# Two samples of a stream through one expert layer at a time, and an order of layers across the samples

## What is computed

```python
x = x + L0_attn(ln(x))   # layer 0: state space scan, 16 heads   (SSM below)
x = x + L0_ffn(ln(x))    # layer 1: feed-forward, token shift     (FFN)
x = x + L1_attn(ln(x))   # layer 2: mamba block, 16 states        (MAM)
x = x + L1_ffn(ln(x))    # layer 3: 8 experts, top 2, gelu        (MOE1)
x = x + L2_attn(ln(x))   # layer 4: linear attention              (ATT)
x = x + L2_ffn(ln(x))    # layer 5: ternary feed-forward          (TER)
x = x + L3_attn(ln(x))   # layer 6: selective scan                (SCAN)
x = x + L3_ffn(ln(x))    # layer 7: 8 experts, top 2, gated silu  (MOE3)
```

## Time and profile before

| | us |
|---|---|
| median of 3 runs | 1499.15 |
| lowest, highest | 1498.88, 1500.82 |
| profiled execution, its own time | 1508.51 |
| profiled execution, span from first to last instruction | 1506.4 |
| PE busy, DVE busy, ACT busy, POOL busy in the span | 1151.1, 920.1, 662.9, 280.6 |

### The profile page before, as it was taken

How to read it: one execution, slowest core, us unless ns; L and a number is a source line. 1 busy time by engine, 2 the same in 40 slices (tenths; PEclk the granted TensorE clock), 3 DMA queues, 4 the chain that set the end, 5 groups by cost and what they waited for, 6 DMA issues and landing times.

```text
span 1506.4 us, 16451 instructions
## 1 busy us (share of the span) xinstructions
PE 1151.1 (76%) x5428; PEld 761.0 (51%) x5428; DVE 920.1 (61%) x2079; ACT 662.9 (44%) x1289; POOL 280.6 (19%) x261
## 2 busy tenths in 40 slices
PE   0988656667869989976897767755867999978774
PEld 0534522233757446666775423433635745547674
DVE  4575679998627384234484778987786355334432
ACT  1532267524634343452452476436943434443321
POOL 1200112425140201203202211213242020020222
PEclk9998767877989998989999868986988999988987
DMA  8000000003564000536540000003513600033763
GB/s 330 0 1 0 1 0 0 0 1 103 188 200 125 20 1 4 172 101 212 172 166 28 7 0 0 0 1 104 172 43 104 200 15 1 0 131 121 271 205 131
DMA packets 57641, 125.50 MB, mean 83 GB/s; under 512 B 5320, under 2 KB 38224, under 8 KB 57168
## 3 DMA queue, kind: packets, MB, share of 16 engines
q1 hardware_dynamic: 52880, 111.14, 22.5%
q0 software_dynamic: 4096, 8.40, 1.7%
q10 hardware_dynamic: 576, 4.87, 0.8%
HBM read 109.31 MB, written 15.07 MB: 83 GB/s over the span
## 4 chain that ended last, share of the span: by engine, by line
PE 46%; DVE 18%; ACT 13%; issue 9%; DMA 8%; POOL 5%; SPq 1%; DVEq 0%; another core or an unknown queue 0%; POOLq 0%; ACTq 0%
PE ps L1739 6%; PE ps L1801 5%; PE ps L1529 5%; DMA expert_ring<-in_e_dram 4%; PE ps L1477 4%; PE ps L1642 3%; PE ps L1712 3%; DVE up L1230 3%; PE ps L1771 2%; POOL slots_dram L639 2%; POOL up L646 2%; PE ps L1582 2%; PE ps L1839 1%; ACT big L862 1%; PE ps L1790 1%
## 5 line engine op out<-in xcount | busy, mean ns | idle before, releaser
L1739 PE MATMUL ps<-big,expert_ring 128*128 128x128 f32 x1440 | 200.1, 289 | 45.6 <-DMA expert_ring<-in_e_dram 18.1
L1739 PEld LDWEIGHTS ps<-big,expert_ring 128*128 128x128 f32 x1440 | 184.6, 201 | 66.7 <-issue 34.5
L587 POOL TENSOR_TENSOR rstd<-ve,nhalf 128x4 f32<-128x4 f32 x44 | 48.2, 1096 | 692.3 <-DVE ve L1024 548.0
L1230 DVE TENSOR_TENSOR_SCAN up<-cv,big 128x512 f32<-128x512 f32 x128 | 151.5, 1223 | 24.7 <-ACT cv L821 18.1
L1642 PE MATMUL ps<-big,consts 128*128 128x512 f32 x256 | 149.1, 713 | 2.2 <-DVE big L1237 2.2
L1712 PE MATMUL ps<-expert_ring,big 128*128 128x128 f32 x960 | 130.0, 279 | 11.5 <-DVE big L1350 6.4
L624 POOL TENSOR_TENSOR big<-big,mt 128x512 f32<-128x512 f32 x64 | 85.1, 1333 | 263.2 <-ACT mt L814 133.6
L1712 PEld LDWEIGHTS ps<-expert_ring,big 128*128 128x128 f32 x960 | 119.3, 194 | 18.4 <-DVE big L1350 7.1
L1659 PE MATMUL ps<-q,row_pick 96*128 96x512 bf16 x128 | 54.5, 441 | 89.3 <-DVE big L1237 57.4
L1801 PE MATMUL ps<-big,weights 128*128 128x512 f32 x256 | 116.1, 598 | 0.8 <-DVE big L1402 0.8
L859 ACT ACTIVATE key<-ps,expert_ring 128x128 f32<-128x128 f32 x240 | 68.6, 369 | 106.2 <-PE ps L1739 94.6
(11 more groups left out here) (249 smaller groups left out, 1990.7 us busy)
## 6 DMA issues: line engine op xcount, KB each, us to landing
expert_ring<-in_e_dram SPq DMA_DIRECT2D x60, 836.0 KB
expert_ring<-in_e_dram SPq DMA_DIRECT2D x60, 578.0 KB
big<-slots_dram SPq DMA_DIRECT2D x24, 256.0 KB, 3.2
results_dram<-mt SPq DMA_DIRECT2D x24, 256.0 KB, 4.5
weights<-in_w_dram ACTq DMA_DIRECT2D x1, 3072.0 KB, 14.8
slots_dram<-big SPq DMA_DIRECT2D x2, 960.0 KB, 16.0
weights<-in_w_dram SPq DMA_DIRECT2D x1, 1600.0 KB, 13.4
big<-slots_dram SPq DMA_DIRECT2D x8, 192.0 KB, 3.8
```

Of the source, the lines that this page charges most:

```text
L1230: dve.tensor_tensor_scan(UP[s][:, j, PAD:PAD + T], CV[s][:, j, :], BIG2[s][:, j, :], 0.0, ALU.mult, ALU.add).then_inc(m_scan[s], 1)
L1739: last = pe.matmul(bank4(s, r if m else b % 2)[:, k, :], ring[:, q % RING, r * T + k * P:r * T + (k + 1) * P], XGT[s][:, b // 4, b % 4 * P ...
```

## The change

**Expert layers take both samples of a stream.** `PAIR = 2`; the two samples' 2048 pairs are sorted into one list of `NBLK = PAIR * 2 * T // P + NE - 1` = 23 blocks in 6 groups (`NGRP`). So 4 expert layers of 23 blocks stand where 8 of 15 stood: 92 blocks instead of 120, of each of the two kinds 46 instead of 60. The norm of the layer (`pair_norm`) and the choice of places work on 8 chunks of tokens instead of 4; the top 2 is found on the logits and the softmax is worked out beside the rest; POOL scatters 16 times in a row and later gathers 16 times in a row, again only when all groups of results are written. Groups 4 and 5 reuse the tiles of groups 0 and 1. Nothing of a stream's next layer can begin before both samples have passed.

```diff
 NE = 8
-NBLK = 2 * T // P + NE - 1
+PAIR = 2
+NBLK = PAIR * 2 * T // P + NE - 1
+NGRP = (NBLK + 3) // 4
...
+GROUPS_AT = {1: (2, 3), 5: (4,), 10: (5,)}
+PLAY = [(0, 0), (0, 1), (1, 0), (2, 0), (1, 1), (2, 1), (3, 0),
+        (4, 0), (5, 0), (4, 1), (5, 1), (6, 0), (6, 1), (7, 0)]
...
         def whole(programs, s):
-            for i in range(s, NB, NS):
-                for program in programs:
-                    yield from program(i)
+            for layer, r in PLAY:
+                if layer in programs:
+                    yield from programs[layer](r * NS + s)
...
                         if label[0] == "x":
                             if n == 0:
-                                sp.wait_ge(scattered[s % NS], 128 * (nth_moe(m, s) + 1))
-                            sp.dma_start(XG[s][:, n, 0:blocks * P].rearrange("p (b n) -> p b n", b=blocks),
+                                sp.wait_ge(scattered[s], 2 * PAIR * NC * 16 * (m + 1))
+                            elif n >= 4:
+                                sp.wait_ge(g.tr[s], g.tr.at(s, n - 4))
+                            sp.dma_start(XG[s][:, n % 4, 0:blocks * P].rearrange("p (b n) -> p b n", b=blocks),
...
+                    for h in range(PAIR):
+                        for r in range(2):
+                            for c in range(NC):
+                                j = r * C2 + h * NC + c
+                                yield
+                                if h == r == c == 0:
+                                    pool.wait_ge(g.pos[s], g.pos.at(s, 0))
+                                    pool.wait_ge(zeroed, 64)
+                                pool.indirect_dma_start(xs_d[s], bass.IndirectOffsetOnAxis(ap=posu[s][:, j:j + 1], axis=0),
+                                                        xh[h][:, c, :], None).then_inc(scattered[s], 16)
...
+            def pair_norm(layer, s):
+                yield
+                after_previous(layer, s)
+                yield from norm(norms[layer], s, (X[s], XH[s]), (X[s + NS], XH2[s]))
...
+                    for c in range(NC):
+                        last = dve.max(top[s][:, h * NC + c, :], lgp[:, c, :])
...
             def gated_sum(m, s):
-                for r in range(2):
-                    yield
-                    dve.wait_ge(gathered[s % NS][r], 64 * (nth_moe(m, s) + 1))
+                for h in range(PAIR):
+                    x = X[h * NS + s]
+                    for r in range(2):
+                        yield
+                        dve.wait_ge(gathered[s][h][r], 64 * (m + 1))
...
-                    yield from turn(g.n, s)
-                    yield from route(m, name, s)
+                    for h in range(PAIR):
+                        yield from turn(g.n, s, h)
+                        logits(m, name, s, h)
+                    yield from route(m, s)
                     for k in range(2):
                         yield from turn_slots(g, s, k)
                     for b in range(NBLK):
-                        if b == 1:
-                            for k in range(2, 4):
-                                yield from turn_slots(g, s, k)
+                        for k in GROUPS_AT.get(b, ()):
+                            yield from turn_slots(g, s, k)
```

More of the change, by code:

```diff
@@ L1037, in norm, with after_previous @@
-                last.then_inc(n.done[s], 1)
+                for h, (src, dst) in enumerate(pairs):
+                    for c in range(NC):
+                        j = h * NC + c
+                        last = dve.tensor_scalar(dst[:, c, :], src[:, c, :], mv[s][:, j, 0:1],
+                                                 rstd[s][:, j:j + 1], ALU.subtract, ALU.mult)
+                    last.then_inc(n.done[s], 1)
+            def after_previous(layer, s):
+                at = PLAY.index((layer, s // NS))
+                if at and not in_general[0]:
+                    before, r = PLAY[at - 1]
+                    dve.wait_ge(x_done[before][s], x_done[before].at(r * NS + s % NS, -1))
@@ new lines, in route @@
+                step(dve.tensor_reduce(used, cnt4[s], AX.X, ALU.add))
+                step(dve.tensor_tensor_scan(ends, ones[:, 0:1].broadcast_to([P, NE]), used, 0.0, ALU.mult, ALU.add))
+                dve.tensor_tensor(past[s], ends[0:1].unsqueeze(1).broadcast_to([1, NBLK, NE]),
+                                  cn("blocks", 1)[:, 0:NBLK].unsqueeze(2).broadcast_to([1, NBLK, NE]), ALU.is_le)
+                step(dve.tensor_tensor(first, ends, used, ALU.subtract))
+                dve.tensor_reduce(whof[s][:, 0:NBLK], past[s], AX.X, ALU.add)
```

387 lines of the change are left out of this document (194 added, 193 removed), and 66 rows, old and new, of the table RUNS.

## The result

The median is 1427.3 us (four runs, 1423.4 to 1431.6), against 1499.0 us for the kernel before beside it (four runs, 1498.2 to 1500.8): a ratio of 0.952, 95% interval 0.949 to 0.955. I had 1456, with 1440 to 1475 around it and a range of 1422 to 1490 that takes in two rivals. The gain is 72 us where I forecast 43, so the time lies in the range but outside 1440 to 1475.

What follows compares the result with a forecast made beforehand. No engine full: PE bounds attention, ternary and experts, DVE paired mamba blocks. Removed blocks free 77 us of PE; walking the new order ends at 1463 against 1506.4, 43 us less, so 1456 from the median; forecast 1440 to 1475, range 1422 to 1490.

Steps and rivals of the forecast that it cites:

- rival 1: Idle time does not grow, or blocks alone run at PE's 2.9 us instead of 3.7; 1422 to 1430, chance 0.20.
- Rival 2: Last 42 blocks run at 4.2 us, or the hand-over at 746 to 837 has such gaps; 1477 to 1490, chance 0.20.
- rival 3: DVE bounds a long mamba stage with nothing to fill it, 254 us instead of 203; 1507 from the median, chance 0.09.
- SSM pairs: State space layers, both samples: first pair 124 us from 33, unchanged up to 157; second 128 us, 2SSM ending at 285.
- Mamba stage: Behind the state space layers: 172 us to 457, then 183 us of DVE at 0.90, 203 us, to 660.
- 3MAM's rest: 0MOE1 beside the 64 of 91 pieces left of 3MAM: 86 us, ending at 746.
- 0MOE1 to 1ATT: From 746: last 0MOE1 blocks to 789, thirteen of 1MOE1 to 837, ten beside 0ATT to 880, gathers and norm to 914.
- ATT, TER, SCAN: Attention, ternary and scan layers, 914 to 1191: 42 us, then 176 us of PE at 0.93 for 189, then 46.
- Last stage: Last experts from 1191: first four blocks by 1276, nineteen more by 1346, 1MOE3 by 1435, 28 us behind them: 1463.
- The ring does not keep up: Blocks that run alone: each late weight load costs its wait and a slow block; the sum keeps 3.7 us a block.
- my 41 intervals: Last stage: 19 intervals of 0MOE3's blocks alone and 22 of 1MOE3's, at 3.7 us each.
- Costed at nothing: Clearing more scratch lists (3 us if in the open), changed routing arithmetic (at most 2 us a layer), fewer weight loads.

Runs made afterwards that it cites:

- two exchange runs: Kernel before with the new table's order of pieces in the first state space pair: 1489.8 us; changed kernel with the old order there: 1445.0 us.
- the kernel whose last stage is unedited: Kernel before with the new table's order of pieces in the first state space pair alone: 1489.8 us, ratio 0.995.

## Why the prediction was right, and where it was off

**Sign, range and rivals.** Faster came as forecast, and the time is in the range of 1422 to 1490, but only because the range holds rival 1; the forecast itself, 1440 to 1475, missed it. The idea behind the sum did not come true: that PE gives up 77 us and idle time eats nearly half of it, since the blocks no longer fill the stages where DVE is the bound. By the sum PE would have been idle for 1463 - (1151 - 77) = 389 us; it was 341, after 355. PE gave up 65 us and all of it is seen in the time. Rival 1 was nearest in its number (1422 to 1430) and in its first condition, that idle time doesn't grow. Its other condition, blocks alone at PE's pace of 2.9 us, did not come: they ran at 3.3 to 3.5. Rival 2 (4.2 us) and rival 3 (a mamba stage at 0.72 of DVE) did not come, though rival 3 had the right place: that stage was the one slower than my sum. The 36 us between my end of 1463 and the measured 1427 are -25 in the SSM pairs, +22 in the mamba stage, -18, -11 and -4 in the three parts behind.

**The term that was mis-sized: the SSM pairs.** I took 124 us for the first, because nothing of it is edited, and 128 for the second. They took 115 and 112; 2SSM ends at 260 instead of 285. "Up to 157 us nothing differs" is the sentence that failed. The table of the order differs there, and I had it before me (41 pieces of 1SSM beside 0SSM before, 56 after) and read it only for the later stages. The two exchange runs give 8 and 18 us for it. For the second pair I went up from the value before me "since 3SSM starts from the end of 1SSM"; the row shows the contrary, PE at 97.96 of 112 us.

**Mamba stage.** 260 to 444 took 184 us where I had 172; 444 to 647 took 203, as forecast; 3MAM's rest took 96 us for 86. In the first part DVE's load was 156.7 us (18.26 + 138.47) where I took over 145.8, and that is 11 of its 12 us. About half of the 11 is more work: 245 instructions after 229, among them eight norm statistics (L1200) of 5 us that in the kernel before fall ahead of this stretch. The other half is longer instructions: the scans and other SBUF to SBUF instructions of one stream now stand more often beside the POOL product of the other, 1287 ns a scan over the whole kernel after 1223. I had costed them by the old stage and had no term for how they meet. The 10 us of 3MAM's rest weren't taken apart. A slip that matters little: 42 of 91 pieces are 0.46 of a block and not 0.43, which makes a mamba block 87 us of DVE and not 88.

**0MOE1 to 1ATT.** 150 us from 743 to 893, where I had 168. By parts, with the forecast in brackets: 41 us to the last result of 0MOE1 (43), 11 to the first of 1MOE1 (16), 34 for twelve more blocks (32), 38 for the ten beside 0ATT (43), 27 from the last result to the end of the sum (34). Four of the five parts were shorter than I had them, none by more than 7 us; where I could not see a wait I had taken it long.

**ATT, TER, SCAN.** 893 to 1159, 266 us, where I had 277. The ends, 42 and 46 us, were as forecast; between them 178 us passed instead of 189, since PE was at 0.98 of 893 to 1131 and I had taken 0.93.

**Last stage.** 268 us after 272. The parts were off and made up for each other, again with the forecast in brackets: the fourth result of 0MOE3 90 us behind the end of 2SCAN (85), nineteen more blocks 65 us (70), 12 to the first result of 1MOE3 (8), 22 blocks 73 (81), and 28 from the last result, with 16 gathers, to the end (28). "The ring does not keep up" was right, as the runs with half the load and with doubled matmuls show, but the price that I gave it, 3.7 us a block, belongs to one execution of the kernel before. The ten and the fourteen intervals that I read it from, first in that profile and then in the kernel whose last stage is unedited (columns as in the earlier trace rows):

```profile
1388.30:1424.60 36.30, 28.68 (x240) 26.56 (x238) 18.27 (x88) 13.69 (x40) 7.76 (x8) 1.00 0.77 268
1436.50:1488.30 51.80, 41.26 (x316) 39.77 (x314) 19.81 (x76) 14.87 (x52) 6.51 (x7) 0.90 0.63 213
...
1379.50:1411.60 32.10, 28.20 (x240) 26.45 (x238) 18.12 (x87) 13.66 (x40) 7.74 (x8) 1.00 0.85 290
1424.90:1470.10 45.20, 37.73 (x316) 35.83 (x314) 19.73 (x76) 14.83 (x52) 6.26 (x7) 1.00 0.74 243
```

The same blocks took 3.6 and 3.7 us each in the one and 3.2 in the other. So the 3.7 holds most of the 9.4 us above the median that I had noted and not traced; nor was a low clock common to blocks that run alone, since the first of these stretches had 1.00 even in that profile. With 3.2 us my 41 intervals would have been 131 us instead of 152; they took 138. By the rule that the Trainium skill (TensorE: Matmul & The Clock Gate, Part 1: The HAM clock gate) gives, a busy array has the full rate; the trace agrees, at 0.97 and 0.98 in the last two stretches of the changed kernel, though its ring kept up no better (29.5 us of waits in 39 blocks, 18.9 in 23 before). What limited the blocks then was the transfer.

**Costed at nothing.** The longer clearing of the scratch lists is not seen: the first layer begins at 33 us as before.

## What to carry to other kernels

When an in-order table of pieces is made anew, its stretches are not those of before even where no layer is edited; read the new table against the old one first, stretch by stretch. The worth of work that is taken out is the worth of the place where it stood: in the old order a block cost some 2.7 us in the last stage and 0.6 on the average of the others, and PE's sum of 77 us did not say which. A profiled execution above the median has its surplus somewhere: look for the stretch before a pace is taken from it. Ahead of a stretch that waits for weights, ask for its bound by halving the transfer: here it is worth 21 us, while a load that is only moved forward is worth nothing.

## What was not expected of the hardware

That POOL's product costs DVE this much: of 64 products of 1.38 us seven eighths taken away give 29 us of 1427, with 23 us of it in DVE's own instruction times. Of the large groups of a mamba block it hits the one whose operands are all in SBUF, the scans, few of them and those by up to 1.5 us (median 1208, longest 2721 ns), and leaves those with an operand in PSUM at 1210 to 1212 and 680 to 681 ns.
